# Staging a whole tile, and storing it in five larger pieces with one of them cut by rows

## The chip, the cores and the metric

One NeuronCore of one Trainium2 chip runs the kernel. The metric is device microseconds (us) of one execution. The kernel before takes 692.0 us, the median of three runs (691.38 to 692.28).

## What is computed

```python
xi = x[:, pi, :]            # all pairs (i, j), i < j, of 32 fields: 496 pairs
xj = x[:, pj, :]
proj = jnp.einsum('bpd,pod->bpo', xi, W)
return proj * xj            # x: (2048, 32, 64), W: (496, 64, 64), all float32
```

For each of 2048 batch rows and each pair (i, j), field i is projected by the pair's own 64x64 matrix and multiplied, element by element, with field j. The output has 2048 x 496 x 64 float32 values, 260 MB, and nearly all traffic is its store.

## The kernel before

The batch is cut into 16 tiles of 128 rows, one row for each partition. The weights lie in `w_sb` for the whole run. For a tile, TensorE turns x (16 transposes, the item `"turn"`, done for the next tile between steps 9 and 10), then multiplies it with the weights in 21 steps. A step fills two PSUM halves, `proj[b][0]` and `proj[b][1]`, and b alternates. VectorE multiplies the first half with field j into `staged`; of the second half, some steps are VectorE's too, and for the others ScalarE copies it to `staged` and GpSimd (POOL) multiplies it there in place (`pool_steps`).

The steps form 11 groups (g0 to g10) of 61, 57, 53, 49, 45, 41, 37, 33, 54, 38 and 28 pairs. A group is a contiguous range of output columns, 256 bytes for each pair in each row. SyncE (SP) issues one store for each group, in order, as soon as the engines that fill it are done. A semaphore `stored[k]` counts the stores of staging buffer k, and the writers wait on it in `slot_free` before they fill the buffer again. There are nine buffers: g9 shares the buffer of g4, and g10 that of g5 (`SHARED_SLOTS`), 430 pairs in all:

```python
SHARED_SLOTS = {9: 4, 10: 5}
...
slot_pairs = [max(group_range(g)[1] for g in range(len(groups)) if slot_of[g] == k) for k in range(slots)]
```

So g9 of a tile can be filled only when g4 of the same tile has been stored.

The first tile (number 0) and the last (15) are written out in code; tiles 1 to 14, the inner ones, are a loop of two tiles (odd, then even). While tile t is computed, ScalarE issues the load of x for tile t+1 (1 MB, `load_x`, before step 3) on its own DMA queue (q10 in the profile; SP's is q1).

The lines that the prediction speaks of are L180 to L183 (SP waits for a group, then issues its store), L213 (POOL's multiply), L249 and L250 (ScalarE waits for a filled half and copies it), L284 (the matmuls) and L326 (VectorE's multiply).

Of the kernel before, what the change touches and what calls it, by code (L numbers as in the profile page):

```python
# [9 lines left out]
P = 128  # L10
# [3 lines left out]
LOAD_BEFORE = 3  # L14
WARM_UP = 16

SHARED_SLOTS = {9: 4, 10: 5}


def pair_index(i, j, fields):  # L20

    return i * (2 * fields - i - 1) // 2 + (j - i - 1)
# [49 lines left out]
def field_pair_project(nc, x, w, ident, out, fields, dim):  # L72
    batch = x.shape[0]
    tiles = batch // P
    steps, groups = plan(fields, dim)
# [10 lines left out]
    def items(tile):  # L86


        for n, item in enumerate(last_tile if tile.last else whole_tile):
            yield item, (1 + n) % 2, tile.number * per_tile + (1 + n) // 2  # L90


    pool_steps = [s for s in range(len(steps) - 1) if s % 3 != 2]
    group_of = {s: g for g, group in enumerate(groups) for s in group}

    def group_range(g):
        segments = [seg for s in groups[g] for unit in steps[s] for seg in unit]
        first = min(pair_index(i, j, fields) for i, j, _ in segments)
        assert sum(n for _, _, n in segments) == max(
            pair_index(i, j, fields) + n for i, j, n in segments) - first  # L100
        return first, sum(n for _, _, n in segments)

    slot_of = [SHARED_SLOTS.get(g, g) for g in range(len(groups))]
    slots = len(groups) - len(SHARED_SLOTS)
    assert sorted(set(slot_of)) == list(range(slots))
    slot_uses = [slot_of.count(k) for k in range(slots)]
    slot_pairs = [max(group_range(g)[1] for g in range(len(groups)) if slot_of[g] == k) for k in range(slots)]


    ends = {s: max(w_at[i] + (j - i - 1 + n) * dim for i, j, n in steps[s][0]) for s in range(len(steps))}  # L110
# [8 lines left out]
    def each_tile(eng, emit):  # L119
        emit(Tile(0, 0, 0))  # L120
        with eng.Fori(0, (tiles - 2) // 2) as t:  # L121
            emit(Tile(2 * t + 1, 1, t))
            emit(Tile(2 * t + 2, 0, t + 1))
        emit(Tile(tiles - 1, 1, tiles // 2 - 1, last=True))

    with ExitStack() as ctx:  # L126
        def sb(name, shape, dt=F32):
            return ctx.enter_context(nc.sbuf_tensor(name, shape, dt))

        def sem(name):  # L130
            return ctx.enter_context(nc.semaphore(name))
# [4 lines left out]

        x_t = [sb(f"x_t{h}", [P, fields // 2, P]) for h in range(2)]
        ident_sb = sb("ident_sb", [P, P])
        staged = [sb(f"staged{k}", [P, slot_pairs[k] * dim]) for k in range(slots)]

        proj = [[ctx.enter_context(nc.psum_tensor(f"proj{b}{h}", [P, UNIT], F32)) for h in range(2)]
                for b in range(2)]
# [6 lines left out]
        emptied = [[sem(f"emptied{b}{h}") for h in range(2)] for b in range(2)]  # L149

        pool_scaled = [sem(f"pool_scaled{g}") for g in range(len(groups))]
        stored = [sem(f"stored{k}") for k in range(slots)]

        block = ctx.enter_context(nc.Block())

        def slot_free(eng, tile, g):

            k = slot_of[g]
            before = [h for h in range(g) if slot_of[h] == k]
            if not (tile.first and not before):  # L160
                eng.wait_ge(stored[k], tile.number * 16 * slot_uses[k] + 16 * len(before))

        def staged_part(s, i, j, n):
            g = group_of[s]
            to = (pair_index(i, j, fields) - group_range(g)[0]) * dim
            return staged[slot_of[g]][:, to:to + n * dim]

        @block.sync
        def _(sp):
            def emit(tile):  # L170
                where = {item: (b, use) for item, b, use in items(tile)}
                for g, group in enumerate(groups):
                    first, n = group_range(g)


                    pooled = any(s in pool_steps for s in group)
                    if pooled and g == 0:
                        sp.wait_ge(pool_scaled[g], tile.number + 1)
                    b, use = where[group[-1]]
                    sp.wait_ge(emptied[b][group[-1] not in pool_steps], use + 1)  # L180
                    if pooled and g > 0:
                        sp.wait_ge(pool_scaled[g], tile.number + 1)  # L182
                    sp.dma_start(out[bass.ds(tile.number * P, P), first * dim:(first + n) * dim],  # L183
                                 staged[slot_of[g]][:, 0:n * dim]).then_inc(stored[slot_of[g]], 16)

            half = fields * dim // 2
            sp.dma_start(x_sb[0][:, 0:half], x[0:P, 0:half]).then_inc(x_first_loaded[0], 16)
            sp.dma_start(w_sb[:, w_cuts[0]:w_cuts[1]], w[:, w_cuts[0]:w_cuts[1]]).then_inc(w_loaded[0], 16)
            sp.dma_start(x_sb[0][:, half:], x[0:P, half:]).then_inc(x_first_loaded[1], 16)
            for c in range(1, len(w_cuts) - 2):  # L190
                sp.dma_start(w_sb[:, w_cuts[c]:w_cuts[c + 1]], w[:, w_cuts[c]:w_cuts[c + 1]]
                             ).then_inc(w_loaded[c], 16)

            c = len(w_cuts) - 2
            sp.dma_start(w_sb[0:dim, w_cuts[c]:w_cuts[c + 1]], w[0:dim, w_cuts[c]:w_cuts[c + 1]]
                         ).then_inc(w_loaded[c], 16)
            sp.dma_start(x_sb[1][:], x[P:2 * P, :]).then_inc(x_loaded[1], 16)

            each_tile(sp, emit)
            for k in range(slots):  # L200
                sp.wait_ge(stored[k], 16 * slot_uses[k] * tiles)

        @block.gpsimd
        def _(pool):
# [16 lines left out]
        @block.scalar  # L221
        def _(act):
            act.dma_start(ident_sb[:], ident).then_inc(ident_loaded, 16)

            def turned_out(b, use, to):
                for h in range(2):
                    act.wait_ge(filled[b][h], use + 1)
                    nc.scalar.activation(x_t[to][:, h * (UNIT // P):(h + 1) * (UNIT // P), :].rearrange(  # L228
                        "p k b -> p (k b)"), proj[b][h][:], ACT.Copy).then_inc(emptied[b][h], 1)

            def load_x(tile):

                _, b, use = list(items(Tile(tile.number - 1, 1 - tile.parity, None)))[-1]

                act.wait_ge(emptied[b][1], use + 1)
                act.wait_ge(pool_scaled[group_of[pool_steps[-1]]], tile.number)
                act.dma_start(x_sb[1 - tile.parity][:], x[bass.ds((tile.number + 1) * P, P), :]
                              ).then_inc(x_loaded[1 - tile.parity], 16)

            def emit(tile):  # L240
                for item, b, use in items(tile):
                    if item == LOAD_BEFORE and not tile.first and not tile.last:
                        load_x(tile)
                    if item == "turn":
                        turned_out(b, use, 1 - tile.parity)
                    elif item in pool_steps:
                        (i, j, n), = steps[item][1]
                        slot_free(act, tile, group_of[item])
                        act.wait_ge(filled[b][1], use + 1)  # L249
                        nc.scalar.activation(staged_part(item, i, j, n), proj[b][1][:, 0:n * dim],  # L250
                                             ACT.Copy).then_inc(emptied[b][1], 1)

            turned_out(0, 0, 0)
            each_tile(act, emit)

        @block.tensor
# [53 lines left out]
        @block.vector  # L310
        def _(dve):
            def emit(tile):
                if tile.first:
                    for h in range(2):
                        dve.wait_ge(x_first_loaded[h], 16)
                for item, b, use in items(tile):
                    if item == "turn":
                        continue
                    slot_free(dve, tile, group_of[item])
                    for h in range(2):  # L320
                        if h and item in pool_steps:
                            continue
                        dve.wait_ge(filled[b][h], use + 1)
                        segments = steps[item][h]
                        for (i, j, n), at in zip(segments, place(segments, dim)):
                            last = nc.vector.tensor_tensor(  # L326
                                staged_part(item, i, j, n), proj[b][h][:, at:at + n * dim],
                                x_sb[tile.parity][:, j * dim:(j + n) * dim], ALU.mult)
                        last.then_inc(emptied[b][h], 1)

            each_tile(dve, emit)
# [30 lines left out]
```

## Time and profile before

| | |
|---|---|
| median of three runs | 692.0 us |
| the profiled execution's own time | 692.27 us |
| its span (first to last recorded work) | 690.5 us |
| TensorE busy | 597.8 us (87%) |
| VectorE busy | 415.0 us (60%) |
| POOL busy | 390.7 us (57%) |
| ScalarE busy | 205.4 us (30%) |
| moved by DMA | 285.15 MB, mean 413 GB/s |
| HBM written | 260.05 MB |

A share of busy time over the span does not say which engine sets the end. To see that, one asks which engine never waits for another, and what the others wait for. [...]

### The profile page before, as it was taken

What the parts mean: (1) busy time and instruction counts of PE and PEld (TensorE: products, weight loads), DVE (VectorE), ACT (ScalarE), POOL (GpSimd) and SP (SyncE); (2) the same over time, 40 slices, a digit from 0 to 9 for tenths busy, and PEclk for the clock granted to TensorE, in tenths of its full rate; (3) what the DMA queues carried; (4) which work ended last, traced back from release to release, by engine and by line L of the source; (5) the groups of instructions that cost most, each with busy time, mean ns of one, the idle gap of its engine ahead of it and who ended that gap; (6) DMA issues with size and microseconds to landing.
All of it is one profiled execution on the core that took longest, in us unless ns stands there. A gap on an engine that the chain in (4) does not pass through costs nothing.

```text
span 690.5 us, 8403 instructions
## 1 busy us (share of the span) xinstructions
PE 597.8 (87%) x2704; PEld 372.9 (54%) x2704; DVE 415.0 (60%) x528; ACT 205.4 (30%) x257; POOL 390.7 (57%) x228
## 2 busy tenths in 40 slices
PE   6889979799797989979799797988979799797972
PEld 4556646466464555646466464645646466464641
DVE  0656646576574756647576474856747576474851
ACT  2322414233241332414223241322414224141320
POOL 0745738457474655738557374755738557374651
PEclk9998989899897998989989898997989989898995
DMA  8999999999999999999999999999999999999897
GB/s 332 386 430 425 431 427 429 426 428 427 423 427 429 392 417 411 427 426 407 428 407 431 406 427 428 412 425 376 424 423 405 428 415 423 414 423 427 357 422 316
DMA packets 29754, 285.15 MB, mean 413 GB/s; under 512 B 3312, under 2 KB 3440, under 8 KB 7216
## 3 DMA queue, kind: packets, MB, share of 16 engines
q1 hardware_dynamic: 27584, 270.28, 93.3%
q10 hardware_dynamic: 2160, 14.75, 5.8%
q8 instruction: 5, 0.08, 0.0%
q14 instruction: 5, 0.04, 0.0%
HBM read 24.97 MB, written 260.05 MB: 413 GB/s over the span
## 4 chain that ended last, share of the span: by engine, by line
DMA 37%; POOL 26%; issue 22%; PE 10%; ACT 2%; DVE 1%; POOLq 0%; SPq 0%; DVEq 0%; ACTq 0%
DMA out_dram<-staged 36%; POOL staged L213 26%; PE proj L284 9%; ACT staged L250 2%; DVE staged L326 1%; DMA ident_sb<-ident_dram 1%; PE proj L301 1%; POOLq L212 0%; PE proj L262 0%; ACT x_t L228 0%; SPq L183 0%; POOLq L121 0%; ACTq L249 0%; DVEq L126 0%; SPq L182 0%
## 5 line engine op out<-in xcount | busy, mean ns | idle before, releaser
L284 PE MATMUL proj<-w_sb,x_t 64*128 64x512 f32 (+7 forms) x2432 | 562.3, 564 | 72.5 <-DVE staged L326 70.1
L326 DVE TENSOR_TENSOR staged<-proj,x_sb 128x1024 f32<-128x1024 f32 (+7 forms) x528 | 415.0, 828 | 264.5 <-PE proj L284 187.0
L213 POOL TENSOR_TENSOR staged<-staged,x_sb 128x1024 f32<-128x1024 f32 (+4 forms) x224 | 390.5, 1755 | 284.6 <-ACT staged L250 283.8
L284 PEld LDWEIGHTS proj<-w_sb,x_t 64*128 64x128 f32 x2432 | 339.2, 205 | 288.5 <-issue 132.1
L250 ACT ACTIVATE staged<-proj 128x1024 f32<-128x1024 f32 (+4 forms) x224 | 172.8, 787 | 453.0 <-PE proj L284 344.6
L262 PEld LDWEIGHTS proj<-ident_sb,x_sb 128*128 128x128 f32 x256 | 30.4, 150 | 10.2 <-issue 7.6
L262 PE MATMUL proj<-ident_sb,x_sb 128*128 128x128 f32 x256 | 34.1, 290 | 1.9 <-DMA x_sb<-x_dram 1.9
L228 ACT ACTIVATE x_t<-proj 128x1024 f32<-128x1024 f32 x32 | 31.2, 1022 | 13.7 <-PE proj L262 12.2
L301 PE MATMUL proj<-ident_sb 128*128 128x128 f32 x16 | 3.7, 425 | 5.7 <-DMA ident_sb<-ident_dram 5.7
L301 PEld LDWEIGHTS proj<-ident_sb 128*128 128x128 f32 x16 | 3.3, 227 | 5.7 <-DMA ident_sb<-ident_dram 5.7
L228 ACT ACT_TABLE_LOAD x1 | 1.3, 1283 | 1.2 <-PEq L356 1.2
L356 POOL MEMSET const-float32-0.0<- 128x1 f32 x1 | 0.1, 98 | 0.2 <-issue 0.2
L356 POOL MEMSET const-bfloat16-1.0<- 128x1 bf16 x1 | 0.1, 101 | 0.0
L356 POOL MEMSET const-uint8-127<- 128x1 uint8 x1 | 0.1, 101 | 0.0
L356 POOL MEMSET const-float32-1.0<- 128x1 f32 x1 | 0.1, 98 | 0.0
## 6 DMA issues: line engine op xcount, KB each, us to landing
out_dram<-staged SPq DMA_DIRECT2D x16, 1952.0 KB, 11.4
out_dram<-staged SPq DMA_DIRECT2D x16, 1824.0 KB, 14.2
out_dram<-staged SPq DMA_DIRECT2D x16, 1728.0 KB, 17.3
out_dram<-staged SPq DMA_DIRECT2D x16, 1696.0 KB, 14.8
out_dram<-staged SPq DMA_DIRECT2D x16, 1568.0 KB, 14.3
out_dram<-staged SPq DMA_DIRECT2D x16, 1440.0 KB, 15.7
out_dram<-staged SPq DMA_DIRECT2D x16, 1312.0 KB, 15.6
out_dram<-staged SPq DMA_DIRECT2D x16, 1216.0 KB, 13.8
```

Of the source, the lines that this page charges most:

```text
L213: last = nc.gpsimd.tensor_tensor(product, product, x_sb[tile.parity][:, j * dim:(j + n) * dim], ALU.mult)
L228: nc.scalar.activation(x_t[to][:, h * (UNIT // P):(h + 1) * (UNIT // P), :].rearrange("p k b -> p (k b)"), proj[b][h][:], ACT.Copy).then_i ...
L250: nc.scalar.activation(staged_part(item, i, j, n), proj[b][1][:, 0:n * dim], ACT.Copy).then_inc(emptied[b][1], 1)
L262: last = nc.tensor.transpose(proj[b][h][:, n * P:(n + 1) * P], x_sb[of][:, k * P:(k + 1) * P], ident_sb[:])
L284: last = nc.tensor.matmul(proj[b][h][:, at:at + width], x_t[tile.parity][half, i // 2, :], w_sb[half, col:col + width], start=True, stop=True)
L301: nc.tensor.transpose(proj[1][0][:, 0:P], ident_sb[:], ident_sb[:])
L326: last = nc.vector.tensor_tensor(staged_part(item, i, j, n), proj[b][h][:, at:at + n * dim], x_sb[tile.parity][:, j * dim:(j + n) * dim], ...
L356: nc = bacc.Bacc("TRN2", target_bir_lowering=False, num_devices=1)
```

## The change

Five things change together.

1. The nine staging buffers become five, which hold a whole tile (496 pairs) and share nothing: `MERGED` puts g0 and g1 in the first (118 pairs), g2 and g3 in the second (102), g4 to g6 in the third (123), g7 and g8 in the fourth (87), g9 and g10 in the fifth (66).
2. In tiles 1 to 14, SP issues one store for each buffer, in place of 11 stores a tile. Tiles 0 and 15 keep 11 pieces.
3. In every odd tile (1, 3, ... 15) g9 and g10 are stored apart, and g10 (28 pairs) goes as two transfers: rows 0 to 119, then rows 120 to 127.
4. VectorE and ScalarE wait once for each buffer and tile (except in tile 0), where they waited once for each step.
5. An area of the on-chip memory that the compiler sets aside for DMA descriptors is 1 KB a partition, which makes room for the larger staging. Only DMAs that GpSimd issues use it, and there are none here.

```diff
-SHARED_SLOTS = {9: 4, 10: 5}
+MERGED = [[0, 1], [2, 3], [4, 5, 6], [7, 8], [9, 10]]
+SPLIT_GROUP = 10
+SPLIT_ROWS = 120
+DMA_SCRATCH = 1024
...
-        staged = [sb(f"staged{k}", [P, slot_pairs[k] * dim]) for k in range(slots)]
+        staged = [sb(f"staged{k}", [P, n * dim]) for k, (_, n) in enumerate(slot_range)]
...
-        def slot_free(eng, tile, g):
-            k = slot_of[g]
-            before = [h for h in range(g) if slot_of[h] == k]
-            if not (tile.first and not before):
-                eng.wait_ge(stored[k], tile.number * 16 * slot_uses[k] + 16 * len(before))
+        def slot_free(eng, tile, k):
+            if not tile.first:
+                more = 2 * (SPLIT_GROUP in MERGED[k])
+                eng.wait_ge(stored[k], tile.half * 16 * (2 + more)
+                            + 16 * (tile.parity + len(MERGED[k]) - 1))
...
-                for g, group in enumerate(groups):
-                    first, n = group_range(g)
+                fine = tile.first or tile.last
+                for these in ([[g] for g in range(len(groups))] if fine
+                              else MERGED[:-1] + [[g] for g in MERGED[-1]] if tile.parity else MERGED):
+                    k, g = slot_of[these[0]], these[-1]
+                    first, n = group_range(these[0])[0], sum(group_range(h)[1] for h in these)
...
-                    sp.dma_start(out[bass.ds(tile.number * P, P), first * dim:(first + n) * dim],
-                                 staged[slot_of[g]][:, 0:n * dim]).then_inc(stored[slot_of[g]], 16)
+                    at = (first - slot_range[k][0]) * dim
+                    split = these == [SPLIT_GROUP] and tile.parity
+                    for row, rows in ((0, SPLIT_ROWS), (SPLIT_ROWS, P - SPLIT_ROWS)) if split else ((0, P),):
+                        sp.dma_start(out[bass.ds(tile.number * P + row, rows), first * dim:(first + n) * dim],
+                                     staged[k][row:row + rows, at:at + n * dim]).then_inc(stored[k], 16)
...
-                    slot_free(dve, tile, group_of[item])
+                    k = slot_of[group_of[item]]
+                    if item == groups[MERGED[k][0]][0]:
+                        slot_free(dve, tile, k)
```

On SP, the end of an odd inner tile read as follows before (the last three stores, g8, g9 and g10; `pool_scaled` and `emptied` are the semaphores of the engines that fill them, and 128x1792 is rows by elements of a row).

```order
L183 ISA [waits pool_scaled8,emptied11]
L183 DMA out_dram<-staged 128x3456
L180 REGISTER_ALU
L183 ISA [waits pool_scaled9,emptied10]
L183 DMA out_dram<-staged 128x2432
L180 REGISTER_ALU
L183 ISA [waits emptied01]
L183 DMA out_dram<-staged 128x1792
```

It reads as follows after the change, from the merged store of g7 and g8 on.

```order
L195 ISA [waits pool_scaled8,emptied11]
L195 DMA out_dram<-staged 128x5568
L189 REGISTER_ALU
L195 ISA [waits pool_scaled9,emptied10]
L195 DMA out_dram<-staged 128x2432
L189 REGISTER_ALU
L195 ISA [waits emptied01]
L195 DMA out_dram<-staged 120x1792
L195 ISA
L195 DMA out_dram<-staged 8x1792
```

The stores of g7 and g8 have become one, and the last store two that follow each other without a wait.

On VectorE, the last two groups of an inner tile read as follows before: the first row of g9 waits for `stored4`, the count of the buffer that g4 also uses, and g10 for `stored5`.

```order
L323 REGISTER_ALU [waits stored4]
L326 TENSOR_TENSOR staged4<-proj00,x_sb1 128x704 [waits filled00]
L326 TENSOR_TENSOR staged4<-proj10,x_sb1 128x576 [waits filled10,stored4]
L323 REGISTER_ALU [waits stored5]
L326 TENSOR_TENSOR staged5<-proj00,x_sb1 128x448 [waits filled00]
```

After the change the same rows read:

```order
L342 REGISTER_ALU [waits stored4]
L345 TENSOR_TENSOR staged4<-proj00,x_sb1 128x704 [waits filled00]
L345 TENSOR_TENSOR staged4<-proj10,x_sb1 128x576 [waits filled10]
L342 REGISTER_ALU
L345 TENSOR_TENSOR staged4<-proj00,x_sb1 128x448 [waits filled00]
```

`staged4` is now a buffer of g9 and g10 alone, so the one wait left is for the stores of the previous tile.

## Rows read from the trace of the kernel before

**Rows 1.** The page, part 1 and 2: busy time, and DMA in 40 slices
```profile
PE 597.8 (87%) x2704; PEld 372.9 (54%) x2704; DVE 415.0 (60%) x528; ACT 205.4 (30%) x257; POOL 390.7 (57%) x228
DMA  8999999999999999999999999999999999999897
```

**Rows 2.** Stretches of DMA: us, busy of five engines, PEclk, DMA share, GB/s
```profile
74.00:228.00 154.00, 134.73 (x617) 83.88 (x617) 93.15 (x121) 46.71 (x59) 87.00 (x52) 0.90 1.01 427
228.00:231.00 3.00, 3.00 (x18) 1.98 (x15) 2.30 (x2) 0.92 (x1) 2.98 (x2) 1.00 0.86 278
...
686.00:688.00 2.00, 0.00 (x0) 0.00 (x0) 0.00 (x0) 0.00 (x0) 0.00 (x0) 0.50 0.10 43
688.00:690.50 2.50, 0.00 (x0) 0.00 (x0) 0.00 (x0) 0.00 (x0) 0.00 (x0) 0.50 0.03 11
```

**Rows 3.** The chain that ended last: start us, us from issue to full landing
```profile
201.81 16.10 DMA out_dram<-staged
244.48 14.92 DMA out_dram<-staged
285.71 15.23 DMA out_dram<-staged
...
450.86 16.13 DMA out_dram<-staged
```

**Rows 4.** ScalarE's wait for the buffer of g4 and g9, three of sixteen tiles
```profile
218.00 1.19 ACT L250 ACTIVATE staged<-proj 128x640 f32<-128x640 f32 x2 [7.32 <-DMA out_dram<-staged]
259.50 1.19 ACT L250 ACTIVATE staged<-proj 128x640 f32<-128x640 f32 x2 [6.13 <-DMA out_dram<-staged]
467.09 1.19 ACT L250 ACTIVATE staged<-proj 128x640 f32<-128x640 f32 x2 [7.35 <-DMA out_dram<-staged]
```

**Rows 5.** The page, part 3: queue, packets, MB, share of 16 engines' span
```profile
DMA packets 29754, 285.15 MB, mean 413 GB/s; under 512 B 3312, under 2 KB 3440, under 8 KB 7216
q1 hardware_dynamic: 27584, 270.28, 93.3%
q10 hardware_dynamic: 2160, 14.75, 5.8%
```

**Rows 6.** Stretch with the weight load of 64 rows, and the one behind it
```profile
25.00:28.00 3.00, 3.00 (x16) 1.59 (x14) 2.18 (x4) 1.51 (x2) 2.26 (x2) 1.00 1.01 205
28.00:31.00 3.00, 1.97 (x10) 0.84 (x6) 2.42 (x3) 0.92 (x1) 2.95 (x2) 1.00 1.06 438
```

**Rows 7.** One tile's stretch: the same columns as rows 2
```profile
115.00:156.00 41.00, 36.26 (x170) 22.75 (x168) 25.64 (x33) 12.74 (x16) 24.17 (x15) 0.92 1.01 427
```

**Rows 8.** TensorE by form, first at granted clock 1.00, then mostly at 0.50
```profile
L284 PE MATMUL proj<-w_sb,x_t 64*128 64x384 f32 x4 | 1.6, 483 | 0.0
...
L284 PE MATMUL proj<-w_sb,x_t 64*128 64x384 f32 x2 | 1.6, 925 | 0.0
```

More of the change, by code:

```diff
@@ L101, in group_range @@
         return first, sum(n for _, _, n in segments)
[L103 to L107, printed above, removed]
+    slot_of = [next(k for k, merged in enumerate(MERGED) if g in merged) for g in range(len(groups))]
+    slots = len(MERGED)
+    slot_range = [(group_range(m[0])[0], sum(group_range(g)[1] for g in m)) for m in MERGED]
     ends = {s: max(w_at[i] + (j - i - 1 + n) * dim for i, j, n in steps[s][0]) for s in range(len(steps))}
@@ L154, in field_pair_project @@
         block = ctx.enter_context(nc.Block())
-        def slot_free(eng, tile, g):
-            k = slot_of[g]
-            before = [h for h in range(g) if slot_of[h] == k]
-            if not (tile.first and not before):
-                eng.wait_ge(stored[k], tile.number * 16 * slot_uses[k] + 16 * len(before))
+        def slot_free(eng, tile, k):
[3 more added lines that the diff above has]
+                            + 16 * (tile.parity + len(MERGED[k]) - 1))
         def staged_part(s, i, j, n):
-            g = group_of[s]
-            to = (pair_index(i, j, fields) - group_range(g)[0]) * dim
-            return staged[slot_of[g]][:, to:to + n * dim]
+            k = slot_of[group_of[s]]
+            to = (pair_index(i, j, fields) - slot_range[k][0]) * dim
+            return staged[k][:, to:to + n * dim]
         @block.sync
@@ L171, in emit @@
                 where = {item: (b, use) for item, b, use in items(tile)}
-                for g, group in enumerate(groups):
-                    first, n = group_range(g)
[L176 to L182, printed above, removed]
-                    sp.dma_start(out[bass.ds(tile.number * P, P), first * dim:(first + n) * dim],
-                                 staged[slot_of[g]][:, 0:n * dim]).then_inc(stored[slot_of[g]], 16)
+                fine = tile.first or tile.last
[3 more added lines that the diff above has]
+                    first, n = group_range(these[0])[0], sum(group_range(h)[1] for h in these)
+                    pooled = [h for h in these if any(s in pool_steps for s in groups[h])]
+                    if pooled and these[0] == 0:
+                        sp.wait_ge(pool_scaled[pooled[-1]], tile.number + 1)
+                    b, use = where[groups[g][-1]]
+                    sp.wait_ge(emptied[b][groups[g][-1] not in pool_steps], use + 1)
+                    if pooled and these[0] > 0:
+                        sp.wait_ge(pool_scaled[pooled[-1]], tile.number + 1)
+                    at = (first - slot_range[k][0]) * dim
[3 more added lines that the diff above has]
+                                     staged[k][row:row + rows, at:at + n * dim]).then_inc(stored[k], 16)
             half = fields * dim // 2
@@ L200, in _ @@
             for k in range(slots):
-                sp.wait_ge(stored[k], 16 * slot_uses[k] * tiles)
+                stores = tiles - 2 + 2 * len(MERGED[k])
+                stores += tiles - 1 if SPLIT_GROUP in MERGED[k] else 0
+                sp.wait_ge(stored[k], 16 * stores)
         @block.gpsimd
@@ L247, in emit @@
                         (i, j, n), = steps[item][1]
-                        slot_free(act, tile, group_of[item])
+                        k = slot_of[group_of[item]]
+                        if item == min(s for s in pool_steps if slot_of[group_of[s]] == k):
+                            slot_free(act, tile, k)
                         act.wait_ge(filled[b][1], use + 1)
@@ L318, in emit @@
                         continue
-                    slot_free(dve, tile, group_of[item])
+                    k = slot_of[group_of[item]]
+                    if item == groups[MERGED[k][0]][0]:
+                        slot_free(dve, tile, k)
                     for h in range(2):
@@ L355 @@
     }
-    nc = bacc.Bacc("TRN2", target_bir_lowering=False, num_devices=1)
+    nc = bacc.Bacc("TRN2", target_bir_lowering=False, num_devices=1,
+                   dynamic_dma_scratch_size=DMA_SCRATCH)
     aps = [nc.dram_tensor(n, a.shape, F32, kind="ExternalInput").ap() for n, a in arrays.items()]
```

## The prediction

> **What bounds the kernel now.** First the page's busy shares: TensorE 87%, and the DMA engines at 9 tenths in all slices but the first and one near the end [rows 1]. Neither proves a bound, so the next view is DMA by stretches. From 74 to 228 us the mean share is 1.01 and 427 GB/s move [rows 2]: for 154 us no DMA engine has time to spare, while compute can afford waits of up to 7.35 us a tile on a store [rows 4]. So DMA is the bound, and compute is gated by it.
>
> But which DMA engine? A tile moves 128 x 496 x 256 bytes out and 128 x 8192 in, 17.30 MB; at 427 GB/s that is 40.5 us. The tiles do not come at that pace. In the chain that ended last, adding each piece's length to its start gives the times at which the store of g4 has fully landed: 217.91, 259.40, 300.94 and, four tiles later, 466.99 [rows 3], which is 41.5 us a tile each time. ScalarE is released by them [rows 4]. The times of issue (the starts of the same rows) are not so even: 42.67 us apart, then 41.23. Between the first two lies a stretch, 228 to 231 us, in which the mean share falls to 0.86 and 278 GB/s [rows 2]. DMA engines stood idle there, and the next landing is still not late. So full landing is set by an engine that was busy all through. The end says the same: from 686 to 688 us the mean share is 0.10, then 0.03 over 2.5 us [rows 2]. One engine of sixteen is 0.0625, so at the end little more than one engine is at work.
>
> I read this as one late DMA engine. It carries 1.081 MB of a tile in 41.5 us, 26.06 GB/s. The mean is 427/16 = 26.69, so the other fifteen run at 26.73 GB/s, 40.46 us a tile. The difference is 1.04 us a tile. The trace's views do not name the engine.
>
> **The change, part by part.** The working is against the profiled execution, 692.27 us (span 690.5 us); the median of the runs shown is 692.0, so 0.3 us below.
>
> *Rows moved off one engine.* The packets of q1 number 27584 [rows 5]. 176 stores of 128 rows, 3 loads of x and 12 of weights with 128 rows, one of weights with 64: that is 24512 rows, and 192 transfers with 16 small packets each are 3072, together 27584. So a row is one packet, and 128 rows are 8 for each of 16 engines. 120 rows cannot be shared evenly by 16; by 15 they can, 8 each. If that is what happens, one engine gets none of g10 in the eight odd tiles. A row of g10 is 7168 bytes, 0.268 us at 26.7 GB/s, and 8 of them 2.15 us. The engine left out gains 8 x 2.15 = 17.2 us. If it is the late one, it ends at 692.3 - 17.2 = 675.1.
>
> The Trainium skill (DMA: Bandwidth & Descriptors, "Why a DMA increments its semaphore by 16") says that a transfer runs on the largest number of engines up to 16 that divides its rows, the lowest-numbered first: 15 for 120 rows, with the last engine left out, and 8 for 8 rows. The same page ("Latency and other measured facts") has engines 7 and 15 usually slower, though it lays that to DMAs that GpSimd issues, which this kernel does not have. No row here shows either.
>
> *The other fifteen.* They become the bound. The span from 74 us holds (690.5 - 74)/41.5 = 14.9 tiles, and at 1.04 us each they would end 15.5 us sooner, at 676.8. The last 8 rows go somewhere: one packet more on each of eight engines, 0.27 us, in eight tiles 2.1 us: 678.9.
>
> *Fewer packets.* An even inner tile has 6 transfers fewer, 48 row packets and 6 small ones on each engine; an odd one 39 and 4. Over 14 tiles that is about 680 packets on an engine. Their bytes stay, and what a packet costs beside its bytes no row shows. From below it is nothing. From above: q1's packets took 93.3% of 16 x 690.5 us [rows 5], 10308 us for 270.28 MB. At the best stretch, 438 GB/s or 27.4 per engine [rows 6], the bytes alone are 9873 us, which leaves 16 ns a packet. I take 5 ns, nearer the lower end since that remainder also holds contention: 3.4 us of 0 to 10.7. Now 675.5.
>
> *Engines on each other's rows.* A transfer of 128 rows runs at full rate with eight rows to each engine. One with fewer rows need not. The only one here is the weight load of 64 rows, 0.26 MB, worth 0.61 us at 427 GB/s. It lies in 25 to 28 us, where the share is 1.01 but only 205 GB/s move; just behind it 438 GB/s [rows 6]. 3.0 x (1 - 205/427) = 1.56 us are lost, 2.5 times its own length. If the 120 rows are dealt to engines in another way than the 128 rows of the stores around them, two engines can want the same part of the on-chip memory. The cost of a split is from nothing (the 128-row row) to 2.5 x 2.15 = 5.5 us (the 64-row row). 120 is an eighth of the way from 128 to 64, which gives 0.7; I take 0.5 us, as neighbours that drift apart stop meeting. Eight splits are 4.0 us: 679.5.
>
> The Trainium skill (SBUF — State Buffer, "Door 1: The DMA port swizzle") speaks against the change here: partitions reach memory over 16 ports, partitions 0 to 63 over only 8 of them. The 205 GB/s fits. By that rule rows 0 to 7 lie on two ports, so 15 engines with 8 neighbouring rows each would meet in pairs. Where they start together they run at half rate for the length of the store, 2.15 us a split, and the four-to-a-port reads of rows 120 to 127 add up to 0.8 us: 675.5 + 23.6 = 699.1. That is the slower rival below.
>
> *Whole-tile staging.* Before, g9 waits until g4 of its own tile has landed. Compute then stands, and g0 of the next tile comes late, which is the 0.86 stretch. After, a buffer is refilled after its own stores of the previous tile, with 378 pairs and a load of x ahead in the queue: 13.4 MB, 31.5 us. To refill the first buffer takes 118/496 of a tile's compute. TensorE is busy 36.26 us in a tile at mean clock 0.92 [rows 7], 33.4 us at clock 1.00, so 7.9 us; at half clock, where a 64x384 matmul takes 925 ns and not 483 [rows 8], 15.9 us; POOL's last multiplies add some 3 us. So the store is issued over 12 us before the queue runs dry. I cost it at nothing: the late engine never ran dry, so it gains nothing either, but it is needed for the fifteen, which would otherwise be held back each tile.
>
> *Merging and waiting once.* Issuing later delays nothing while the queue has 12 us in hand. Behind SP's merged wait only later stores are queued. The load of x shares engines with packets twice as long and lands some us later; it is needed only by the transposes after step 9, and compute has 40.5 - 33.4 = 7 us a tile to spare. The wait that the split adds on g10's store is none: SP issues the second part at once. Startup and tile 0: nothing, the queue is full. Tile 15 keeps its eleven pieces.
>
> Sum: 692.3 - 15.5 + 2.1 - 3.4 + 4.0 = 679.5 us.
>
> **Rivals.**
> (1) *Meeting engines eat it, slower.* Each split costs all fifteen engines c us; time = 675.5 + 8c. It decides at c = 2.1, above which nothing is left. For it: the 205 GB/s, and a bound of 5.5. Against: 120 is nearly 128, and the fifteen drift apart. With c near 3, 699 us. Chance 0.11.
> (2) *The late engine is not the one left out.* It stays the bound and gets only the saved packets: 692.3 - 3.4 = 688.9, or 691.0 if it is one of the eight with a packet more. For it: nothing in the trace says which engine is late. Or c is between 1.2 and 2.1, 685 to 692. Chance 0.24, a fifth of it no change.
> (3) *The split does nothing*: 120 rows are dealt so that the late engine keeps its share; 689 as well. Within the chance of (2).
> (4) *TensorE becomes the bound.* 33.4 us passes 40.5 at a mean clock of 0.82; it is 0.92 now with one long wait a tile, and the change makes five short waits. At 0.75 a tile takes 44.5 us, 14 tiles 56 us more than 40.5: 735. Against: the clock falls only when TensorE waits, so when it has time. Chance 0.02.
>
> **How the numbers follow.** The forecast (c under 1.2) has 0.63, its own range 671 to 686: down to the upper packet bound and c near 0 with (675.5 - 7.3 = 668 is the very end), up to c = 1.2. The full range takes in rival (2): 671 to 691. Left out are (1) and (4), 0.13, and the ends. What this kernel's measurement tells from no change is about 0.2%, 1.4 us. Faster: 0.63 and four fifths of (2), 0.82. Same 0.05. Slower 0.13, (1) and (4).
>
> **What would show it.** Right: landings of a buffer's last store 40.3 to 41.0 us apart; no stretch under 400 GB/s between tiles except in the few us around the splits; and DMA share at the end falling from near 1 to 0 in under 2 us, as the engines end together. Waits on stores spread over five places a tile. Wrong: a tail of one engine still over 3 us long and 41.3 to 41.5 us a tile (rival 2); share near 1 with 250 to 350 GB/s after each odd tile (rival 1); the share under 0.9 with TensorE never idle at clock under 0.82 (rival 4).

## The result: 707.1 us, 2.2% slower

The changed kernel takes 707.1 us, the median of 6 runs (705.1 to 708.5); the kernel before took 691.7 us in the runs beside it. The ratio is 1.022, with a 95% interval of 1.020 to 1.024. The forecast was 679.5 us.

The page of the changed kernel, parts 1 to 3, answers to [rows 1] and [rows 5]:

```profile
span 705.2 us, 7889 instructions
...
PE 584.3 (83%) x2704; PEld 361.8 (51%) x2704; DVE 408.7 (58%) x528; ACT 208.2 (30%) x257; POOL 391.7 (56%) x228
...
DMA  8999999999999999999999999999999999999991
...
DMA packets 18721, 285.14 MB, mean 404 GB/s; under 512 B 2136, under 2 KB 2264, under 8 KB 5144
...
q1 hardware_dynamic: 16552, 270.28, 92.7%
```

The same bytes move in a third fewer packets, the DMA engines are still busy in every slice but the first and the last, and yet the mean rate is 404 GB/s where it was 413. So the queues did not run dry. The engines were busy longer with the same bytes: the packets took 97.7% of 705.2 us, 689 us in the mean of the engines, where they took 99.1% of 690.5, 684 us.

Stretches near the end, in the columns of [rows 2]:

```profile
685.00:690.00 5.00, 0.00 (x0) 0.00 (x0) 0.00 (x0) 0.00 (x0) 0.00 (x0) 0.50 0.67 208
690.00:700.00 10.00, 0.00 (x0) 0.00 (x0) 0.00 (x0) 0.00 (x0) 0.00 (x0) 0.50 0.21 82
700.00:705.20 5.20, 0.00 (x0) 0.00 (x0) 0.00 (x0) 0.00 (x0) 0.00 (x0) 0.50 0.05 20
```

A share of 0.21 over 10 us is about three engines of sixteen. Before, the tail of few engines was some 3 us long; here it is about 14 us. The engines ended further apart, where the forecast wanted them to end together. The load of x also came later: 16.4 us from issue to landing in the median, with eight waits of TensorE on it, 35.0 us in all (9.0 us and 1.9 us before). The experiments below tell whether that matters.

How the time is spread over the tiles is seen where VectorE is released by a store, at the first piece of the third buffer. These are its rows in the timeline (start us, length; idle before it and what ended it), for tiles in turn:

```profile
143.94 2.35 DVE L345 TENSOR_TENSOR staged<-proj,x_sb 128x512 f32<-128x512 f32 x3 [5.72 <-DMA out_dram<-staged]
...
184.60 2.35 DVE L345 TENSOR_TENSOR staged<-proj,x_sb 128x512 f32<-128x512 f32 x3 [5.99 <-DMA out_dram<-staged]
...
229.33 2.35 DVE L345 TENSOR_TENSOR staged<-proj,x_sb 128x512 f32<-128x512 f32 x3 [5.72 <-DMA out_dram<-staged]
...
269.93 2.35 DVE L345 TENSOR_TENSOR staged<-proj,x_sb 128x512 f32<-128x512 f32 x3 [5.97 <-DMA out_dram<-staged]
...
314.40 2.36 DVE L345 TENSOR_TENSOR staged<-proj,x_sb 128x512 f32<-128x512 f32 x3 [5.66 <-DMA out_dram<-staged]
```

The steps are 40.7, 44.7, 40.6 and 44.5 us. Every other one, with a cut store in it, is 4 us longer, the other ones are under the 41.5 us of [rows 4]. A pair of tiles takes 85.3 us where it took 83.0.

### The profile page after: what moved, and what is told of

Read it like the earlier page. It is cut to its first block, busy times and chain, and to the rows that moved or that the text cites. A ratio compares the mean times of both kernels' runs of the same rounds, so it can differ in the third digit from the quotient of the medians.

```text
span 705.2 us, 7889 instructions
## 1 busy us (share of the span) xinstructions
PE 584.3 (83%) x2704; PEld 361.8 (51%) x2704; DVE 408.7 (58%) x528; ACT 208.2 (30%) x257; POOL 391.7 (56%) x228
## 2 busy tenths in 40 slices
DMA packets 18721, 285.14 MB, mean 404 GB/s; under 512 B 2136, under 2 KB 2264, under 8 KB 5144
## 4 chain that ended last, share of the span: by engine, by line
DMA 50%; PE 37%; POOL 3%; issue 2%; DVE 2%; SPq 1%; ACT 1%; ACTq 0%; POOLq 0%; DVEq 0%
DMA out_dram<-staged 30%; PE proj L301 29%; DMA x_sb<-x_dram 20%; PE proj L279 7%; POOL staged L228 3%; DVE staged L345 2%; ACT staged L267 1%; SPq L203 1%; ACTq L252 0%; SPq L207 0%; SPq L195 0%; SPq L201 0%; SPq L199 0%; SPq L200 0%; POOLq L227 0%
## 5 line engine op out<-in xcount | busy, mean ns | idle before, releaser
L345 DVE TENSOR_TENSOR staged<-proj,x_sb 128x1024 f32<-128x1024 f32 (+7 forms) x528 | 408.7, 827 | 265.1 <-PE proj L301 158.9
L301 PE MATMUL proj<-w_sb,x_t 64*128 64x512 f32 (+7 forms) x2432 | 528.2, 540 | 19.9 <-DVE staged L345 18.5
L301 PEld LDWEIGHTS proj<-w_sb,x_t 64*128 64x128 f32 x2432 | 310.4, 190 | 233.0 <-issue 128.6
L279 PE MATMUL proj<-ident_sb,x_sb 128*128 128x128 f32 x256 | 53.8, 397 | 62.0 <-DMA x_sb<-x_dram 35.0
L279 PEld LDWEIGHTS proj<-ident_sb,x_sb 128*128 128x128 f32 x256 | 48.2, 212 | 70.9 <-DMA x_sb<-x_dram 39.9
L243 ACT ACTIVATE x_t<-proj 128x1024 f32<-128x1024 f32 x32 | 32.4, 1023 | 44.7 <-PE proj L279 44.6
## 6 DMA issues: line engine op xcount, KB each, us to landing
x_sb<-x_dram ACTq DMA_DIRECT2D x14, 1024.0 KB, 16.4
```

The lines of the kernel that those rows point to most:

```text
L279: last = nc.tensor.transpose(proj[b][h][:, n * P:(n + 1) * P], x_sb[of][:, k * P:(k + 1) * P], ident_sb[:])
L301: last = nc.tensor.matmul(proj[b][h][:, at:at + width], x_t[tile.parity][half, i // 2, :], w_sb[half, col:col + width], start=True, stop=True)
L345: last = nc.vector.tensor_tensor(staged_part(item, i, j, n), proj[b][h][:, at:at + n * dim], x_sb[tile.parity][:, j * dim:(j + n) * dim], ...
```

## The experiments

Ratios are to the kernel before in the same runs.

**Cut and merging apart.** Four kernels. The first is the changed kernel without the cut, and with g9 and g10 of an odd tile in one store again (the counts that `slot_free` waits for, left out here, follow):

```diff
-                              else MERGED[:-1] + [[g] for g in MERGED[-1]] if tile.parity else MERGED):
+                              else MERGED):
...
-                    split = these == [SPLIT_GROUP] and tile.parity
+                    split = False
```

> The changed kernel without the cut by rows: five buffers, five stores in every inner tile. T1 (engines on each other's rows: the cut costs 4 to 5 us in every odd tile, as the landings of the first buffer in the changed kernel, 45.0 and 40.2 us apart in turn, suggest): without it the late engine has only fewer packets, 686 to 690 us, landings about 41.2 us apart in every tile. T2 (the large, late stores and the later x, at which TensorE stands 35 us in the changed kernel, cost the time): 700 to 707 us, the cut hardly matters.

Measured: 686.2 us, ratio 0.992 (0.990 to 0.993). Here VectorE's releases at the third buffer are even:

```profile
142.73 2.35 DVE L342 TENSOR_TENSOR staged<-proj,x_sb 128x512 f32<-128x512 f32 x3 [6.11 <-DMA out_dram<-staged]
...
183.89 2.35 DVE L342 TENSOR_TENSOR staged<-proj,x_sb 128x512 f32<-128x512 f32 x3 [6.48 <-DMA out_dram<-staged]
...
225.05 2.35 DVE L342 TENSOR_TENSOR staged<-proj,x_sb 128x512 f32<-128x512 f32 x3 [6.47 <-DMA out_dram<-staged]
...
266.23 2.35 DVE L342 TENSOR_TENSOR staged<-proj,x_sb 128x512 f32<-128x512 f32 x3 [6.47 <-DMA out_dram<-staged]
```

41.16 us each time. So the cut costs 20.9 us on five buffers (707.1 - 686.2; some 0.4 us of this, 63 packets at the 7 ns found below, is that g9 and g10 stay apart in odd tiles), and the rest of the change gains 5.2 us (691.5 us for the kernel before beside this run). Near the end of this kernel:

```profile
670.00:675.00 5.00, 0.00 (x0) 0.00 (x0) 0.00 (x0) 0.00 (x0) 0.00 (x0) 0.50 0.11 48
675.00:680.00 5.00, 0.00 (x0) 0.00 (x0) 0.00 (x0) 0.00 (x0) 0.00 (x0) 0.50 0.06 27
680.00:684.80 4.80, 0.00 (x0) 0.00 (x0) 0.00 (x0) 0.00 (x0) 0.00 (x0) 0.50 0.05 20
```

0.06 is one engine of sixteen, 27 GB/s its full rate. It works alone for some 13 us. The late engine of the prediction is plain to see, and the other fifteen are no longer held back to its pace.

The packet records of this trace show in what way it is late. Of the 1792 rows of 26112 bytes, 112, just one engine's share, took over 979 ns, 1003 in the mean, where the median is 968. Of those of 30208 bytes, 114 took 1172 ns in the mean, where the median is 1119. Followed back from the end of the trace, they are the last engine's. Its rows took 14.8 us more than the medians in 13.6 tiles, those of the two engines that end next 4.3 and 2.7 us. But when it works alone at the end, its rows take no more than the others' medians (366 ns for 9728 bytes). So it is slowed only while there is other work, and not slow by itself.

The second has the five buffers with all eleven stores, without merging or cut:

```diff
-                fine = tile.first or tile.last
+                fine = True
```

(and the counts that `slot_free` waits for).

> Five buffers that hold a whole tile, but eleven stores a tile and no cut: the staging alone. T1: the late engine is busy throughout before and after, so 691 to 692.5 us, and no stretch with the share at 0.86. T2 (waiting for whole buffers starves the queue): above 695 us.

Measured: 691.2 us, ratio 1.000 (0.999 to 1.001). The staging alone is worth nothing that can be told, which fits a late engine that never ran dry. The 5.0 us between this kernel and the last are the merging: 14 tiles x 54 packets are 756 fewer on the late engine, 7 ns each in the mean. Not all of that is a fixed price. Where the late engine works alone in the last trace, its rows follow each other after 268 ns (7168 bytes) to 513 ns (13824 bytes). A line through the two leaves 4 ns a row beside the bytes, and a completion packet, the small one behind an engine's rows of a store, takes 6 ns. For 48 rows and 6 completions a tile that makes 3.3 us. What the rest is stays open.

The third is the kernel before with the cut alone:

```diff
+                    split = g == 10 and tile.parity
+                    for row, rows in ((0, 120), (120, 8)) if split else ((0, P),):
...
```

> The kernel before, with only the last 28 pairs of every odd tile stored as 120 and 8 rows. T1: slower than before by most of what the changed kernel lost and a little more, 702 to 715 us. T2: the late engine is relieved and nothing else is hurt, 676 to 690 us.

Measured: 702.2 us, ratio 1.014 (1.013 to 1.016). The cut costs 10.7 us here, 1.3 us for each of eight. ScalarE's releases, to be held against [rows 4]:

```profile
261.05 1.19 ACT L254 ACTIVATE staged<-proj 128x640 f32<-128x640 f32 x2 [6.22 <-DMA out_dram<-staged]
...
304.28 1.19 ACT L254 ACTIVATE staged<-proj 128x640 f32<-128x640 f32 x2 [7.66 <-DMA out_dram<-staged]
...
346.02 1.19 ACT L254 ACTIVATE staged<-proj 128x640 f32<-128x640 f32 x2 [7.56 <-DMA out_dram<-staged]
...
388.57 1.19 ACT L254 ACTIVATE staged<-proj 128x640 f32<-128x640 f32 x2 [7.16 <-DMA out_dram<-staged]
```

The steps are 43.2, 41.7 and 42.6 us, none of them under 41.5.

The fourth asks which engine is late:

```diff
+            for n in range(1, 17):
+                sp.dma_start(scratch[16 * n - 16:16 * n - 16 + n, 0:n * 64], w_sb[0:n, 0:n * 64]).then_inc(ladder, 16)
+            sp.wait_ge(ladder, 256)
```

> The kernel before, with sixteen tiny stores added at the very end, of 1 to 16 rows and as many times 256 bytes a row, to a scratch area. It finds which engine is late: a store of n rows puts one packet on each of n engines, so the smallest packet on the engine that ends last tells its place. If it is the sixteenth it has one packet of 4096 bytes after its last row of g10; if it is among the first eight it has nine or more. If the sixteenth is late, the relief in the changed kernel was aimed right and was eaten; if another is, the relief was wasted. Time within 1 us of before plus 2 us for the tail.

Measured: 693.1 us, one run. The tiny packets are told from each other by their size: the trace has one of 256 bytes, two of 512 and so on up to sixteen of 4096. So the engine that ends last tells its place by the smallest tiny packet that it has. These are starts from the packet records, the latest packet of each store, in us before the trace's last packet. The second and third lines belong to two runs further below:

```
rows of the tiny store          4       5       6       7
kernel before                -4.45   -2.45   -2.39   -2.33
five buffers without a cut  -12.04   -1.31   -1.25   -1.18
changed kernel              -16.45   -1.31   -1.25   -1.18
```

Up to 4 rows, no packet is late. From 5 rows on one always is, 2 us behind the others in the first line. So the engine that ends last is the fifth in the order in which small stores take up engines, and not the sixteenth.

**Is it unequal shares, or the dealing of rows?** The kernel before, cut as 112 and 16 rows (the diff is against the cut of 120 and 8):

```diff
-                    for row, rows in ((0, 120), (120, 8)) if split else ((0, P),):
+                    for row, rows in ((0, 112), (112, 16)) if split else ((0, P),):
```

> The kernel before, with the last 28 pairs of every odd tile stored as 112 and 16 rows: both are divisible by 16, so every engine keeps 8 rows, and none is relieved or loaded more. It tells whether the cost is in unequal shares or in the dealing of rows to engines. T1 (engines meet on each other's rows whenever a store is cut below 128 rows): 697 to 706 us, near the 702.2 of 120 and 8. T3 (the cost comes from the eight extra packets and the small last store alone): 691 to 693 us.

Measured: 701.3 us, ratio 1.014 (1.011 to 1.016). Every engine keeps 8 rows, no row packet is added, and 9.8 us are there, no less than 10.7 as far as the spread of the runs tells (699.5 to 703.8). The control cuts the same stores by columns:

```diff
+                    for at, m in ((0, 14), (14, 14)) if split else ((0, n),):
+                        sp.dma_start(out[bass.ds(tile.number * P, P), (first + at) * dim:(first + at + m) * dim],
+                                     staged[slot_of[g]][:, at * dim:(at + m) * dim]
...
```

> The kernel before, with the last 28 pairs of every odd tile stored as two transfers of 14 pairs and all 128 rows each: one transfer more, as with 112 and 16 rows, 8 row packets more on every engine, but every row stays with the engine that has it now. T1 (a cut by rows costs because rows are dealt to engines in another way): 691 to 692.5 us. T3 (a second small store costs): 698 to 702 us.

Measured: 691.9 us, ratio 1.000 (1.000 to 1.001). Two stores in place of one, and even 8 packets more for each engine, cost nothing that can be told. What costs in these kernels is a store with fewer than 128 rows among stores of 128.

**The same tiny stores on two other kernels**, the changed one and the one without the cut.

> The changed kernel with the sixteen tiny stores of 1 to 16 rows at the end. In the kernel before the engine that ends last takes its first tiny packet from the store of 5 rows, so it is the fifth. If it is the fifth here too, the relief of the sixteenth was simply wasted, and the fifth had one packet more in every odd tile. If another one ends last here, the cut has made a new late engine. Time 707 to 710 us.

> The five-buffer kernel without the cut, with the same tiny stores at the end. The late engine is the fifth again if lateness belongs to the engine; time 686 to 689 us, and the tiny packets of the others some 10 us ahead of it.

Measured: 711.1 and 688.9 us, one run each. The packets are the second and third lines of the table above. The fifth engine ends last in both. Without the cut, all others are ahead of it by over 9 us. With the cut, the seventh and the fifteenth end within 2 us of it (their first tiny packets, of 7 and of 15 rows, start 3.2 and 1.9 us before the end). So the cut makes further engines late. The fifth and the seventh have a ninth row of 7168 bytes, behind the completion packet of their eight; the fifteenth has none. In the trace of the changed kernel shown first, without tiny stores, the last engine has no ninth row either. If the 8-row store goes to the first eight there too, the engine that set the time of that run was not the fifth.

**Does the cost double because of shares?** The changed kernel with 112 and 16 rows:

```diff
-SPLIT_ROWS = 120
+SPLIT_ROWS = 112
```

> The changed kernel with rows 0 to 111 and 112 to 127 as the cut, so that every engine keeps 8 rows and the fifth has no packet more. T5 (the doubled cost of the cut on five buffers, 20.9 us against 10.7 on the kernel before, comes from rows dealt otherwise, met by engines that are now further apart): 701 to 708 us. T6 (it comes from the extra packet of the first eight engines, and from the relief that went to the wrong one): 694 to 698 us, the 686.2 us plus what 112 and 16 cost before, 9.8 us.

Measured: 705.4 us, ratio 1.021 (1.018 to 1.023), 19.2 us above the kernel without a cut. The shares explain at most the 1.7 us to 707.1. The doubling against the kernel before comes with the five buffers. This run also settles the late x: TensorE waits only 5.7 us for it here, and the kernel is almost as slow as the changed one.

The packet records show where the time goes. With the cut, packets take 16.8 us more in the mean of the engines than without it on five buffers, and 9.3 us more on the kernel before. The rows of 7168 bytes in the cut stores have 7.0 of the one (over 272 ns a row) and 5.3 of the other. So most of the doubling is in rows of the other stores. The rows of the cut store themselves, in the changed kernel, tile by tile:

```
odd tile                                    1     3     5     7     9    11    13
first to last row of the store starts, us   7.1  11.9  15.2  18.3  18.7  18.8  18.7
mean of a row, ns                          327   362   380   380   401   409   424
rows of 128 that took over 326 ns           22    33    42    48    53    55    61
```

Up to tile 13, the later the tile, the further apart the engines are at this store, and the slower its rows. In tile 15, where some engines are already done, a row takes 363 ns in the mean. The spread is not all: in the kernel before with this cut, where it is some 12 us in tiles 3 to 13, the same rows take 342 to 435 ns.

**Larger stores.** Three buffers and three stores, in the last tile too, and no cut:

```diff
-MERGED = [[0, 1], [2, 3], [4, 5, 6], [7, 8], [9, 10]]
+MERGED = [[0, 1, 2], [3, 4, 5], [6, 7, 8, 9, 10]]
```

> No cut, and three buffers and stores a tile (171, 135 and 190 pairs), in the last tile too: 16 row packets fewer on every engine in each inner tile, 64 fewer in the last. From 686.2 us for five, which took 54 packets off a tile and gained 5.2 us in 14 tiles, 7 ns a packet: 2.0 us less again, 684.2 us, if a packet costs the late engine a fixed time. If the queue now runs dry (it holds only about 25 us when a buffer comes free, and the refill of 190 pairs takes 13 us at full clock): above 687 us.

Measured: 733.9 us, ratio 1.061 (1.060 to 1.063): a miss. The page, parts 2, 5 and 6:

```profile
DMA  8999999999969989698897998979889799896998
...
L276 PE MATMUL proj<-ident_sb,x_sb 128*128 128x128 f32 x256 | 53.2, 394 | 120.9 <-DMA x_sb<-x_dram 120.9
...
x_sb<-x_dram ACTq DMA_DIRECT2D x14, 1024.0 KB, 21.8
```

The load of x lands 21.8 us after its issue (9.0 us in the kernel before), TensorE waits 120.9 us for it in 14 tiles, and DMA runs dry in between, with shares down to 6 tenths. The store rows beside it are up to 48.6 thousand bytes long (190 pairs). With rows up to 31.5 thousand bytes, in the changed kernel, the load took 16.4 us to land, and with rows up to 15.6 thousand, in the kernel before, 9.0 us. That x has to take its turn behind such rows is my reading of these three.

**Using what is idle at the end.** First the last tile was merged too (`fine = tile.first`).

> Five buffers and five stores in the last tile as well, no cut. In the kernel with eleven stores there, one engine alone is at work for the last 14 us, so issuing the last stores later cannot hurt while its queue is that deep; it saves it 48 row packets and 6 small ones, 0.4 us at 7 ns: 685.8 us against 686.2. If the late engine did run dry it would be slower than 687 us.

Measured: 686.15 us, ratio 0.992 (0.990 to 0.993), no difference from 686.2 that can be told; the 0.4 us expected at 7 ns a packet are not seen. Then part of the last tile was taken from the late engine. 124 rows can be shared evenly by four engines alone:

```diff
+                    cuts = ((0, 128, 0, 18), (0, 124, 18, 48), (124, 4, 18, 48)) \
+                        if tile.last and these == MERGED[-1] else ((0, P, 0, n),)
```

> The same, and 48 of the last 66 pairs of the last tile go as 124 and 4 rows, which only four engines can share evenly: 32 rows of 12288 bytes each on the first four, none on the others. T4 (the fifth engine is the late one, and the others idle 14 us at the end): it is spared 8 packets of 0.46 us, 3.65 us, and the first four end at about 670 + 11 = 681: 682 to 683.5 us. If the late engine were among the first four, 11 us slower, 697 us; if the cut costs as in the middle of the run, 684 to 686 us.

Measured: 689.5 us, ratio 0.997 (0.996 to 0.998), slower than without. In the trace the fifth engine is done 4.9 us before the end, at 682.7 us, but two of the first four then end last. Of the 128 rows of 12288 bytes, 28 took over 0.7 us, up to 2.06, where the median is 0.46. With 30 pairs in place of 48:

> Five buffers, no cut but in the last tile, where 30 of the last 66 pairs (before: 48) go as 124 and 4 rows, to the first four engines alone. With 48 pairs the fifth engine ended some 2 us sooner and two of the first four ended last, with single packets of 12288 bytes that took over 1 us in place of 0.46. With 30 the fifth is spared 8 x 0.28 = 2.3 us by size, and the first four have 24 x 0.18 = 4.2 us less to do than with 48: 683.5 to 686 us. If meeting engines cost the fifth what it was spared: 686 to 687 us.

Measured: 684.2 us, ratio 0.989 (0.987 to 0.990). It is the fastest kernel of the study, 2.0 us under 686.2. The end of it:

```profile
670.00:675.00 5.00, 0.00 (x0) 0.00 (x0) 0.00 (x0) 0.00 (x0) 0.00 (x0) 0.50 0.32 126
675.00:680.00 5.00, 0.00 (x0) 0.00 (x0) 0.00 (x0) 0.00 (x0) 0.00 (x0) 0.50 0.21 85
680.00:682.60 2.60, 0.00 (x0) 0.00 (x0) 0.00 (x0) 0.00 (x0) 0.00 (x0) 0.50 0.04 18
```

From 675 to 680 us a share of 0.21 moves 85 GB/s, where one engine alone moved 27. Sparing the engines from the fifth on moves the end. So the one that sets it is not among the first four, which fits the fifth; this run by itself does not tell the fifth from those behind it.

## Why the prediction was wrong

**DMA is the bound, and one late engine sets the landings: right.** The staging alone changed nothing (691.2 us), though the other engines were no longer held, and without the cut one engine works alone for 13 us.

**"If it is the late one, it ends at 692.3 - 17.2 = 675.1": the step that failed first.** The condition was open, and I gave it nearly two chances in three on no row of the profile. The engine left out is the sixteenth, the late one the fifth. 17.2 us of relief went to an engine that had time, so the term of -15.5 us was nothing. That 120 rows go to 15 engines and 8 rows to 8 is right: the page of the profile counts 2136 packets under 512 B, which is 122 whole transfers x 16 and 8 x (15 + 8). The trace agrees there with the Trainium skill (DMA: Bandwidth & Descriptors, "Why a DMA increments its semaphore by 16 and not by 1"). That the one left out is the sixteenth rests on that section alone, which gives such transfers the lowest-numbered engines.

**"I take 0.5 us, as neighbours that drift apart stop meeting": the step that turned the sign.** A cut cost 1.3 us in sum on the kernel before and 2.6 us on five buffers, within the stated bounds of nothing and 5.5. In the prediction's terms, 8 cuts at 0.5 us and 2.1 us for the ninth rows made 6.1 us, where 20.9 were measured. The reason given for 0.5 does not fit the runs. Engines that drift apart did not stop meeting: at a spread of 18.7 us 61 of 128 rows of the cut store were slow, at 7.1 us 22, and the cost doubled just where the fifteen could run ahead. The interpolation by rows (120 is nearly 128) was wrong as well. 112 and 16 rows, with equal shares, cost no more than 120 and 8 where it would give twice as much, and a cut by columns costs nothing. So in these runs it is not how many rows are missing that counts, but that a store is not one of 128 rows. It fits the rule of the Trainium skill that was weighed (SBUF — State Buffer, "Door 1: The DMA port swizzle"). No run here shows the ports themselves, nor which rows an engine gets, so that two engines then read through one port is argued, not shown. What is shown is that the cut by rows is the cause, and that the engines' own packets take longer with it.

**Fewer packets, 3.4 us: right in kind, too small.** Merging gained 5.0 us over 756 packets, 7 ns each where 5 were taken. The changed kernel merges less in odd tiles, the 680 packets of the prediction.

**Whole-tile staging and single waits at nothing: right.** Compute had time, as the sum said. The load of x came nearer to mattering than I had it, as the 35.0 us of waits show.

The sum as it came out, from 691.5 us for the kernel before beside these runs: nothing for the staging (-0.3 us, within the noise), -5.0 for the merging, +20.9 for the cuts, 707.1 us. Rival (1) had the mechanism, with its relief term wrong: since the late engine was not spared, a cut had only to cost over 5.2/8 = 0.65 us to lose.

What stays open: why the fifth engine is slowed by 1 us a tile while others work, and why a cut costs twice as much on five buffers. That the distance between engines is the cause of the second is my reading of two pairs of kernels and of the rows tile by tile. No run varied that distance alone, and the store rows of five buffers are also longer, which may be the cause as well.

## What to carry to other kernels

When DMA is the bound, ask for the slowest of its sixteen engines and not for the mean: the pace of full landings and the share in the last microseconds show it. Before you take load from one engine, find out which one is late; sixteen tiny stores of 1 to 16 rows at the end name it in one run. Do not cut a store by rows in mid-run without measuring it (each cut cost 1.3 to 2.6 us here, a cut by columns nothing), and merge stores as far as a load that shares the engines still lands in time.

## What the runs showed of the hardware

A DMA engine alone moves 27 GB/s (share 0.06). Alone, it spends 4 ns on a row beside its bytes and starts each row's packet 3 to 4 ns before the one before it ends, which is one reason why shares add up to slightly over 1. With the others at work, 756 packets fewer were worth 5.0 us, 7 ns each. One of the sixteen, the fifth in the order in which small transfers are dealt, was late in all three kernels that were probed for it, one run each, on two chips. One engine in sixteen took 3.6% longer for rows of 26112 bytes than the others (1003 and 968 ns), and no longer when it was alone. A store cut by rows goes with slow packets: in the changed kernel's packet records, a row of 7168 bytes took 272 ns in the median as before, but 369 ns in the mean (288 before) and 1.27 us at most (0.53 before).
